# Self attention with q and k projected features first, and the rotation's halves moved by ScalarE

## What is computed

```python
q = (h @ wq + bq).reshape(b, s, H, HD).transpose(0, 2, 1, 3)     # 16 heads of 128
k = (h @ wk + bk).reshape(b, s, H, HD).transpose(0, 2, 1, 3)
v = (h @ wv + bv).reshape(b, s, H, HD).transpose(0, 2, 1, 3)
q = q * cos + _rotate_half(q) * sin                              # _rotate_half: (-x2, x1)
k = k * cos + _rotate_half(k) * sin
scores = jnp.einsum('bhqd,bhkd->bhqk', q, k) / math.sqrt(HD)
scores = jnp.where(causal[None, None], scores, jnp.finfo(jnp.float32).min)
probs = jax.nn.softmax(scores, axis=-1)
out = jnp.einsum('bhqk,bhkd->bhqd', probs, v)
return out.transpose(0, 2, 1, 3).reshape(b, s, H * HD) @ wo + bo
```

## Time and profile before

| | us |
|---|---|
| median of 3 runs (lowest, highest) | 2274.76 (2271.26, 2274.86) |
| profiled execution | 2266.63 |
| its span, first to last instruction | 2264.7 |
| PE busy over the span | 1838.8 (81%) |
| ACT, DVE, POOL busy | 1260.8, 1126.6, 1057.5 |

### The profile page before, as it was taken

The page is one execution under the profiler, slowest core; times in us unless marked ns, Lnnn a source line. Parts: engine busy times, 40 slices in busy tenths (PEclk is TensorE's granted clock), DMA queues, the critical chain, the costliest instruction groups (busy, mean ns, idle before and its releaser), DMA issues.

```text
span 2264.7 us, 36408 instructions
## 1 busy us (share of the span) xinstructions
PE 1838.8 (81%) x11392; PEld 1605.2 (71%) x11392; DVE 1126.6 (50%) x3244; ACT 1260.8 (56%) x4119; POOL 1057.5 (47%) x1192
## 2 busy tenths in 40 slices
PE   3699998279999999999655554589888988888698
PEld 1487886158888888888555552478777877787598
DVE  1566665555555555555533332544444444444422
ACT  1367675236666666666522222387777777877321
POOL 2333332666657667655445553333333333333255
PEclk9799999589999999999877777699999999999799
DMA  3000000100000000000010000000000000000000
GB/s 102 17 15 15 15 24 19 60 31 15 24 16 15 29 15 15 15 15 10 5 33 16 16 8 28 20 10 8 9 10 10 7 10 10 17 12 17 3 15 24
DMA packets 29213, 42.81 MB, mean 19 GB/s; under 512 B 4704, under 2 KB 18528, under 8 KB 28768
## 3 DMA queue, kind: packets, MB, share of 16 engines
q1 hardware_dynamic: 29024, 40.48, 5.8%
HBM read 36.27 MB, written 4.19 MB: 18 GB/s over the span
## 4 chain that ended last, share of the span: by engine, by line
PE 52%; ACT 13%; DVE 11%; POOL 10%; issue 7%; DMA 1%; POOLq 1%; SPq 0%; ACTq 0%; DVEq 0%
PE pA L444 5%; PE pA L446 5%; PE pA L445 5%; PE pS L878 4%; PE pF L444 4%; PE pF L445 3%; PE pF L446 3%; ACT pA L1427 3%; ACT x_P L1461 3%; PE pF L610 3%; PE pO L897 2%; PE pS L589 2%; POOL moe_tb L1958 2%; PE pT L870 2%; PE pT L887 2%
## 5 line engine op out<-in xcount | busy, mean ns | idle before, releaser
L444 PE MATMUL pA<-Wh,XTh 128*128 128x512 f32 (+1 forms) x768 | 335.9, 437 | 22.3 <-POOLq L120 11.9
L446 PE MATMUL pA<-Wh,XTl 128*128 128x512 f32 (+1 forms) x768 | 292.1, 380 | 0.0
L445 PE MATMUL pA<-Wl,XTh 128*128 128x512 f32 (+1 forms) x768 | 291.5, 380 | 0.0
L439 POOL TENSOR_TENSOR Wl<-RAW,Wh 128x512 fp32r<-128x512 f32 (+3 forms) x96 | 101.9, 1061 | 288.2 <-ACT Wh L432 288.2
L444 PEld LDWEIGHTS pA<-Wh,XTh 128*128 128x128 f32 x768 | 148.8, 194 | 47.2 <-POOLq L120 13.1
L1176 POOL TENSOR_TENSOR f_t<-f_t,f_RB 128x512 f32<-128x512 f32 x128 | 165.0, 1289 | 16.7 <-DVE f_t L1060 16.6
L446 PEld LDWEIGHTS pA<-Wh,XTl 128*128 128x128 f32 x768 | 147.9, 193 | 28.7
L445 PEld LDWEIGHTS pA<-Wl,XTh 128*128 128x128 f32 x768 | 149.1, 194 | 21.1
L1060 DVE TENSOR_TENSOR f_t<-pA,f_sin 128x512 f32<-128x512 f32 x128 | 88.5, 692 | 140.7 <-PE pA L446 99.4
L986 ACT ACTIVATE f_P<-f_P,f_nm 128x128 f32<-128x128 f32 (+1 forms) x256 | 113.6, 447 | 49.6 <-DVE f_nm L1079 49.5
L1583 DVE TENSOR_TENSOR x_OTl<-pO,x_OTh 128x256 fp32r<-128x256 f32 x128 | 54.4, 425 | 169.6 <-ACT x_OTh L1475 169.3
(11 more groups left out here) (233 smaller groups left out, 5996.2 us busy)
## 6 DMA issues: line engine op xcount, KB each, us to landing
RAW<-in_w_f SPq DMA_DIRECT2D x32, 256.0 KB, 2.6
RAW<-in_w_x SPq DMA_DIRECT2D x32, 160.0 KB, 2.2
RAW<-in_w_x SPq DMA_DIRECT2D x32, 128.0 KB, 2.0
RAW<-in_w_ff SPq DMA_DIRECT2D x8, 288.0 KB, 2.8
R<-in_x SPq DMA_DIRECT2D x4, 512.0 KB, 5.8
x_spill<-R SPq DMA_DIRECT2D x1, 2048.0 KB, 7.6
f_bqk<-in_f_b SPq DMA_DIRECT2D x4, 512.0 KB, 3.9
RAW<-in_w_moe SPq DMA_DIRECT2D x8, 256.0 KB, 2.7
```

Of the source, the lines that this page charges most:

```text
L439: pool.tensor_tensor(Wl[slot][:, at], RAW[:, s, 0:cw], Wh[slot][:, at].bitcast(F32), ALU.subtract).then_inc(split_done, 1)
L444: e.matmul(o, ah, bh, start=first, stop=False)
L445: e.matmul(o, ah, bl, start=False, stop=False)
L446: return e.matmul(o, al, bh, start=False, stop=last)
```

## The change

The projections of q and k exchange their operands: the weights are stationary, the tokens stream (256 columns), so features come out on the partitions and no transposes of q and k are needed. `proj(i, n)` for n < 4 is now q (n even) or k (n odd) of two heads for all 256 tokens, as two accumulation groups of 6 matmuls of 256 columns. The halves of a head now lie on different partitions, so VectorE can't exchange them along the free axis: ScalarE does it (`swapped`), with four activations of 64 partitions by 256 for each projection, each reading one half of the partitions of `pA` and writing the other half of `sw`, adding the bias on the way. VectorE adds the bias and multiplies by cos (two scalar_tensor_tensor); it now waits for `sw`, and `taken` still comes from it. GpSimd multiplies by sin and adds. There are no rotated bias tables. qT and kT have two buffers.

```diff
-                    t = n // 2 if n < 4 else n - 4
-                    w0 = WV if n >= 4 else WK * (n % 2)
...
+                    for a in range(2):
+                        o = pA[:, n % 2, a * S:(a + 1) * S]
+                        h = 2 * (n // 2) + a
+                        for k in range(KD):
+                            at = WK * (n % 2) + k * GW + h * HD
+                            w = slice(at, at + HD)
+                            xh, xl = XTh[:, k, b], XTl[:, k, b]
+                            e.matmul(o, Wh[g % 2][:, w], xh, start=(k == 0), stop=False)
+                            e.matmul(o, Wh[g % 2][:, w], xl, start=False, stop=False)
+                            ins = e.matmul(o, Wl[g % 2][:, w], xh, start=False, stop=(k == KD - 1))
...
-                def qk_tr(i, n):
...
-                def qk_ev(i, n):
...
+                def swapped(i, n):
+                    m = NT * i + n
+                    e.wait_ge(q["proj"], NQ * i + n + 1)
+                    e.wait_ge(q["rope"], pos(m - 1))
+                    for a in range(2):
+                        h = (i // 8) * HG + 2 * (n // 2) + a
+                        for r in range(2):
+                            src, dst = slice(r * H2, (r + 1) * H2), slice((1 - r) * H2, (2 - r) * H2)
+                            ins = e.activation(sw[dst, n % 2, a, :], pA[src, n % 2, a * S:(a + 1) * S],
+                                               ACT.Identity, bias=bqk[src, n % 2, h:h + 1])
+                    ins.then_inc(q["sw"], 1)
...
                 for i in range(NI):
...
+                    if one:
+                        swapped(j, 3)
                     p_ev(i, 0)
                     normalise(i, 1)
                     exp(i, 2)
                     o_ev(i, 0)
                     p_ev(i, 1)
                     normalise(i, 2)
-                    if one:
-                        qk_ev(j, 0)
-                        qk_ev(j, 1)
                     exp(i, 3)
                     o_ev(i, 1)
                     p_ev(i, 2)
-                    if one:
-                        qk_ev(j, 2)
-                        qk_ev(j, 3)
                     normalise(i, 3)
+                    if two:
+                        swapped(k, 0)
                     o_ev(i, 2)
                     w_high(i)
+                    if two:
+                        swapped(k, 1)
                     p_ev(i, 3)
                     if one:
                         exp(j, 0)
                         normalise(j, 0)
+                    if two:
+                        swapped(k, 2)
+                    if one:
                         exp(j, 1)
                     o_ev(i, 3)
...
                 def take(i, n):
-                    e.wait_ge(q["proj"], NQ * i + n + 1)
                     if n < 4:
...
+                        e.wait_ge(q["sw"], NT * i + n + 1)
...
+                            ins = e.scalar_tensor_tensor(x[:, a, :], pA[:, n % 2, a * S:(a + 1) * S],
+                                                         bqk[:, n % 2, h:h + 1], cosd[:, :], ALU.add, ALU.mult)
+                        ins.then_inc(q["taken"], 1)
...
                 def rotate(i, n):
...
+                    e.wait_ge(q["sw"], m + 1)
+                    e.tensor_tensor(y, y, bc(sind[:, :], 1, 2), ALU.mult).then_inc(q["swm"], 1)
+                    e.wait_ge(q["swm"], m + 1)
                     e.wait_ge(q["taken"], NQ * i + n + 1)
                     e.tensor_tensor(x, x, y, ALU.add).then_inc(q["rope"], 1)
```

More of the change, by code:

```diff
@@ L808, in self_attention @@
             bias_in = [q["bias0"], q["bias1"]]
[L810 to L812 removed]
             def at_p(i, h):
[L815 to L822, removed]
+                return HG * i + h
             def sp(e):
[L825 to L826 removed]
+                e.dma_start(cosd[:, :], d["cosd"]).then_inc(q["const"], 16)
+                e.dma_start(sind[:, :], d["sind"]).then_inc(q["const"], 16)
                 e.dma_start(mask[:, :], d["mask_f0"]).then_inc(q["const"], 16)
+                e.dma_start(bqk[:, :, :].rearrange("p a n -> p (a n)"), d["f0_bqk"]).then_inc(q["const"], 16)
                 def biases(g):
[L830 to L833, removed]
+                    e.dma_start(bv[:, g % 2, :], d["f0_bv"][g * GW:(g + 1) * GW].partition_broadcast(P)
                                 ).then_inc(bias_in[g % 2], 16)
@@ L864, in qk_tr @@
-                def qk_tr(i, n):
[L865 to L872, removed]
+                    if n >= 4:
+                        for k in range(KD):
+                            cc = slice(WV + k * GW, WV + (k + 1) * GW)
+                            ins = three(e, pA[:, n % 2, :], x_part(XTh, i, k, n - 4), x_part(XTl, i, k, n - 4),
+                                        Wh[g % 2][:, cc], Wl[g % 2][:, cc], k == 0, k == KD - 1)
+                        ins.then_inc(q["proj"], 1)
+                        return
@@ new lines, in proj @@
+                    b = slice((i % B) * S, (i % B + 1) * S)
+                    for a in range(2):
+                        o = pA[:, n % 2, a * S:(a + 1) * S]
+                        h = 2 * (n // 2) + a
+                        for k in range(KD):
+                            at = WK * (n % 2) + k * GW + h * HD
[4 more added lines that the diff above has]
+                            ins = e.matmul(o, Wl[g % 2][:, w], xh, start=False, stop=(k == KD - 1))
@@ L915, in pe @@
                     proj(0, n)
-                for n in range(NT):
-                    qk_tr(0, n)
                 proj(1, 0)
@@ L1006, in w_high @@
                     high_w(e, raw_in, q["hi"], cw_next if g == G - 1 else cw_here, i, i % 2, (g + 1) % 2)
+                e.wait_ge(q["const"], 64)
                 for n in range(NT):
-                    qk_ev(0, n)
+                    swapped(0, n)
+                swapped(1, 0)
                 exp(0, 0)
+                swapped(1, 1)
                 normalise(0, 0)
+                swapped(1, 2)
                 exp(0, 1)
                 for i in range(NI):
-                    j = i + 1
-                    one = j < NI
+                    j, k = i + 1, i + 2
+                    one, two = j < NI, k < NI
+                    if one:
+                        swapped(j, 3)
                     p_ev(i, 0)
@@ L1042, in dve @@
             def dve(e):
[L1043 to L1052, removed]
+                e.wait_ge(q["const"], 64)
                 def take(i, n):
-                    e.wait_ge(q["proj"], NQ * i + n + 1)
                     if n < 4:
[L1057 to L1065, removed]
+                        e.wait_ge(q["sw"], NT * i + n + 1)
+                        e.wait_ge(q["sc"], pos(HG * (i - 1)))
+                        x = (kT if n % 2 else qT)[:, i % 2, 2 * (n // 2):2 * (n // 2) + 2, :]
+                        for a in range(2):
+                            h = (i // 8) * HG + 2 * (n // 2) + a
+                            ins = e.scalar_tensor_tensor(x[:, a, :], pA[:, n % 2, a * S:(a + 1) * S],
+                                                         bqk[:, n % 2, h:h + 1], cosd[:, :], ALU.add, ALU.mult)
+                        ins.then_inc(q["taken"], 1)
                     else:
                         g = i // 8
+                        e.wait_ge(q["proj"], NQ * i + n + 1)
                         e.wait_ge(bias_in[g % 2], 16 * (g // 2 + 1))
@@ L1115, in dve @@
                     one, two = j < NI, k < NI
+                    soft(i, 2)
                     if one:
                         take(j, 3)
-                    soft(i, 2)
-                    if one:
                         take(j, 4)
@@ L1183, in w_low @@
                     low_w(e, q["hi"], q["split"], cw_next if g == G - 1 else cw_here, i, i % 2, (g + 1) % 2)
-                rotate(0, 0)
-                rotate(0, 1)
-                rotated_bias(0, 2)
-                rotate(0, 2)
-                rotated_bias(0, 3)
-                rotate(0, 3)
-                for n in range(NT):
-                    rotate(1, n)
+                for i in range(2):
+                    for n in range(NT):
+                        rotate(i, n)
                 for i in range(NI):
-                    g = i // 8
-                    if g < G - 1 and 2 <= i % 8 < 2 + NT:
-                        rotated_bias(g + 1, i % 8 - 2)
                     w_low(i)
@@ L2279, in layout @@
                                        rows(a[f0 + "wo"][g * GW:(g + 1) * GW])], 1) for g in range(G)])
-    o["f0_b"] = c(np.concatenate([a[f0 + n].reshape(G, 1, GW) for n in ("bq", "bk", "bv")], 1).reshape(-1))
+    o["f0_bv"] = a[f0 + "bv"]
+    o["f0_bqk"] = c(np.concatenate([col(a[f0 + "bq"]), col(a[f0 + "bk"])], 1))
     o["f0_bo"] = a[f0 + "bo"]
```

85 lines of the change are left out of this document (19 added, 66 removed).

## The result

| | before | changed |
|---|---|---|
| median us (lowest, highest), 4 runs each | 2273.01 (2267.23, 2274.86) | 2316.93 (2315.30, 2320.84) |
| profiled execution, its span | 2266.63, 2264.7 | 2316.88, 2315.1 |
| ratio, 95% interval | | 1.020 (1.0177 to 1.0224) |

The account below looks back on a forecast made before the run. PE bound the kernel before; ScalarE's swaps would now lengthen laps: -14.8 + 0 + 29 x 1.33 + 3.34 - 2.0 = +25.1, so 2291.7 us, with 8.1 to the median 2300. Own range 2285 to 2312; 8 in 10: 2257 to 2325.

Parts of the forecast that it names:

- lap: Self attention, end of one item's projection 0 to the next item's: 19.81 us before, 21.14 forecast, 17.86 without PE waits.
- part A: From the end of projection 0 to the item's first `attend`: 9.48 us before, forecast 12.82 through ScalarE's queue.
- A swap is 1.94: ScalarE's four half-height activations per q/k projection: 4 x (0.474 + 0.012) = 1.94 us, without overlap.
- the chain: ScalarE's queue followed instruction by instruction from the end of projection 0 to `attend`, reaching 12.82 us.
- part B: From an item's first `attend` to the end of the next projection 0: 10.33 us before, forecast 8.32 without transposes.
- Start -14.8: Start of self attention: without the bias table and rotated bias tables, the first item runs 14.8 us earlier.
- First lap 0: First lap of self attention: 17.02 us before, 17.05 forecast, so no change.
- rival 4: Self attention laps: VectorE or POOL adds a wait left out, +0.3 to +0.6 a lap, 2309 to 2317 us; chance 0.10.
- Rival 1: ScalarE's swaps: half-height activations overlap after all, lap 19.77 us, time 2259 us; chance 0.13.
- Rival 2: Self attention: PE stays the bound, lap 17.86 us, time 2201 us, needs a swap below about 1.1; chance 0.05.
- Rival 3: TensorE's clock falls to 0.91 in the new gaps, +0.8 us a lap, 2324 us; chance 0.12.
- The signs of being wrong: New profile: swaps following at 0.38, ScalarE idling over 3 us a lap, or PE's 256-column projections over 1.5 us each.

Follow-up runs that it names:

- dma_swap: Changed kernel, but ScalarE evacuates q/k projections with bias at full height and SP's DMAs exchange the halves inside SBUF, complete kernel: 2186.18 us, ratio 0.962.
- full2: Changed kernel with each swap as two activations of 128x256, halves not exchanged: 2193.45 us, 18.16 us a lap.
- reorder: Changed kernel with ScalarE evacuating head 0's probabilities (p_ev) before the item's last swap instead of behind it: 2321.22 us, 22.11 us a lap.
- full4: Changed kernel with each swap as four full-height activations of 128x256, bias pointer kept, halves not exchanged: 2241.69 us, 19.65 us a lap.
- straight4: Changed kernel with each swap as four activations of 64x256 writing the same half they read, so no crossing: 2305.08 us, 21.50 us a lap.
- cross_id: Changed kernel with the four crossing activations of 64x256 as Identity without a bias pointer: 2264.12 us, 20.29 us a lap.

## Why the forecast was right in kind and small in size

- *PE is the bound before, and its work would be 17.86 a lap.* Right: dma_swap and its 17.88. Twelve matmuls of 256 columns take 1.51 (799.76 to 801.27, changed kernel) where 1.49 was forecast.
- *ScalarE sets part A.* Right: full2 and dma_swap take its load away and the loss is gone; reorder only moves the wait.
- *A swap is 1.94.* Right: 1.94, put together from half-height rows without a pointer and full-height rows with one. The Trainium skill ("ScalarE: Activation LUTs", section "What ACT_TABLE_LOAD costs") gives neighbours an overlap of about 93 ns. The trace of full4 has 0.12 at full height (starts 0.36 apart, mean duration 0.479), and between the half-height activations of one swap no run has any.
- *Part A is 12.82.* This is the step that failed in size. In one part A the rows above give 823.01 - 815.30 = 7.71 up to swap 2 (PE leaves projection 0 at 815.30, and swap 0 starts 0.20 later), and 806.93 - 801.10 = 5.83 from swap 2 to `attend`, together 13.5. I had kept the neighbours' prices from the earlier trace rows, with their overlap, for six instructions that stand beside a swap. Each costs 0.12 to 0.14 more, together 0.77 a lap; the swaps, at 1.94 where the chain had 1.96, give a little back, and part B adds 0.05. Over 29 laps that is the 22.8. The earlier trace rows could not have told: its swap ends without overlap, which the forecast has, but w_high behind it keeps its own (0.33 from 211.51 to the next start at 211.84, at a duration of 0.42), and the kernel before has no half-height activation with a bias pointer. The open question was whether the neighbours change too, and no bound or rival of the forecast stood for it.
- *Part B is 8.32 and has room.* Right within 0.1: 806.93 to 815.30 is 8.37.
- *Start -14.8.* Right: -14.95 from PE's first matmul to the first scores; PE's later start takes 1.1 of it, inside the 3 that the forecast allowed.
- *First lap 0.* Wrong by 2.7. ScalarE stands still twice there, 2.5 together: `exp` waits for soft(0, 0), which stands on VectorE behind the take for swap 0, and `normalise` for `recip(0, 0)`, which stands there behind the take for swap 1. It is the kind of wait that rival 4 spoke of, in one lap only.

```profile
470.19 0.40 ACT L966 ACTIVATE f_P<-f_P,f_nm 128x128 f32<-128x128 f32 x1 [1.49 <-DVE f_nm L1055]
...
474.13 0.80 ACT L974 ACTIVATE f_P<-f_P,f_rs 128x128 f32<-128x128 f32 x2 [1.01 <-DVE f_rs L1063]
```

- *Rival 1*: full4 is what it would have been, 19.65 a lap (19.77 in the forecast). *Rival 2*: its condition was the right one, and full2, with a swap of 0.7, comes near to it. *Rival 3*: not in the laps, where the granted clock is 1.00; only in the last matmuls of the block, for about 2 us. *Rival 4*: the measured 2316.93 lies where it would be (2309 to 2317), and above the forecast's own range of 2285 to 2312; but its cause, a wait for VectorE or GpSimd that was left out, is there only in the first lap.
- *The signs of being wrong.* One came true: ScalarE was to idle no more than 3 us a lap, and it idles 3.6 (82.18 of the 500 us). The sign was badly chosen, since the forecast itself had ScalarE occupied for about 17 of 21 us. In part A ScalarE has gaps of 0.26 and 0.23; the others lie in part B, where it waits for PE and VectorE. And the 256-column projections, at 1.51, are at the bound of 1.5.
- The measured difference (43.9) is smaller than that of the profiled spans (50.4): the profiled execution before, 2266.63, lies 6.4 under its median, the one after, 2316.88, at its median. The forecast added 8.1 to get from one profiled execution to a median. Against spans its sum is 25 short, against medians 19: that the forecast's time is not further off is in part the luck of one low profiled execution.

## What to carry to other kernels

Work taken off the bound engine pays only if the engine that gets its replacement can do it where it stands in its order: add up that engine's queue between the release and the next use of the buffer, not its busy share. An engine's price for an instruction includes what it does to the overlap of its neighbours. A move of data across partitions that has a lap of slack belongs on the DMA queues: here 512 half-height activations became 256 full-height ones and 256 transfers, and 44 us lost became 86 won.

## What the runs showed of the hardware

- Activations of 64x256 from PSUM with a bias pointer start 0.48 apart at a duration of 0.47 (changed kernel), against 0.36 apart at full height (full4). In these runs the overlap with the instruction ahead is lost by crossing (0.11 to 0.13, back in straight4), the overlap behind by half height (back in full4), and with a bias pointer the next instruction loses its own too (0.13, back in cross_id), with the one exception shown there.
- Identity and Copy cost the same (20.29 a lap each).
- DMAs of 128 KB between the halves of SBUF, 224 in 500 us, landed in 2.3 us at a DMA share of 0.32. The weights' transfers of 256 KB landed in 2.9 us beside them, against 2.6 in the changed kernel, and no engine waited for them.
